# Tails of the second expert layer on the two partition halves of TensorE

## What is computed

```python
scores = jax.nn.softmax(xf @ gate_w.T, axis=-1)
_, idx = lax.top_k(scores + gate_b, 2)            # 2 of 8 experts for each of 4096 tokens
h = jax.nn.silu((einsum('td,edh->teh', xf, w1) + b1) * (einsum('td,edh->teh', xf, w3) + b3))   # h is 176 wide
oe = jnp.einsum('teh,ehd->ted', h, w2) + b2
y = jnp.einsum('te,ted->td', rw, oe)              # weighted by the two chosen scores
z = _expert(xf, sw1, sb1, sw3, sb3, sw2, sb2)     # one more expert of the same shape, for all tokens
x = x + y + z
```

## Time and profile before

| | |
|---|---|
| median of three runs | 703.93 us (702.35 to 705.06) |
| profiled execution, first to last instruction | 699.0 us |
| TensorE matmul busy | 653.6 us, 94% |
| TensorE weight load busy | 550.9 us, 79% |
| DVE / ACT / POOL busy | 527.0 / 421.3 / 507.5 us |
| mean granted TensorE clock | 0.978 |

### The profile page before, as it was taken

How to read it: one execution, slowest core, us unless ns; L and a number is a source line. 1 busy time by engine, 2 the same in 40 slices (tenths; PEclk the granted TensorE clock), 3 DMA queues, 4 the chain that set the end, 5 groups by cost and what they waited for, 6 DMA issues and landing times.

```text
span 699.0 us, 20550 instructions
## 1 busy us (share of the span) xinstructions
PE 653.6 (94%) x6836; PEld 550.9 (79%) x6836; DVE 527.0 (75%) x1507; ACT 421.3 (60%) x1166; POOL 507.5 (73%) x844
## 2 busy tenths in 40 slices
PE   8899999999988999999988999999899787999998
PEld 6577777777766999999985777777676676999997
DVE  4589999999853566665445789999999578778876
ACT  5567777776545333333444667677674675777773
POOL 5865588668765898887767776888787776777671
PEclk9999999999989999999997999999999999999999
DMA  5490001011423332334311101011121013333375
GB/s 178 112 352 6 10 26 33 26 33 35 159 68 93 116 119 62 95 97 126 88 41 35 32 17 32 29 59 46 35 71 49 32 48 98 103 100 101 94 251 195
DMA packets 45404, 57.69 MB, mean 83 GB/s; under 512 B 11379, under 2 KB 37142, under 8 KB 44630
## 3 DMA queue, kind: packets, MB, share of 16 engines
q1 hardware_dynamic: 36086, 38.12, 18.4%
q0 software_dynamic: 8640, 17.97, 7.6%
q10 hardware_dynamic: 576, 0.29, 0.2%
HBM read 33.77 MB, written 22.08 MB: 80 GB/s over the span
## 4 chain that ended last, share of the span: by engine, by line
PE 38%; DVE 23%; POOL 20%; issue 11%; DMA 2%; ACT 2%; SPq 2%; DVEq 0%; POOLq 0%; ACTq 0%
POOL results L1624 10%; PE S L2059 6%; PE ptp L2078 6%; DVE mx L1061 5%; DVE pr L1062 5%; PE M L1365 4%; PE S L1328 4%; POOL rows L620 3%; PE ptp L1348 3%; PE S L1330 3%; POOL xi L1617 3%; PE M L1416 2%; PE S L2065 2%; PE ptp L1351 2%; SPq L709 1%
## 5 line engine op out<-in xcount | busy, mean ns | idle before, releaser
L620 POOL DMA_INDIRECT rows<-out_rows,posi x128 | 126.9, 991 | 48.5 <-issue 28.5
L803 ACT ACTIVATE pT<-ptp 128x512 f32<-128x512 f32 (+1 forms) x192 | 94.1, 524 | 79.4 <-PE ptp L1348 72.3
L1061 DVE TENSOR_REDUCE mx<-S 128x16 f32<-128x1232 f32 x64 | 91.2, 1425 | 16.4 <-PE S L1330 15.8
L1624 POOL DMA_INDIRECT results<-early,xi x71 | 74.8, 1053 | 31.3 <-DVE early L1688 24.1
L1062 DVE TENSOR_TENSOR pr<-S,mx 128x1232 f32<-128x1232 f32 x64 | 92.2, 1441 | 2.2
L1929 POOL DMA_INDIRECT results<-early,xs x71 | 69.2, 975 | 27.4 <-issue 17.1
L1714 PE MATMUL S<-early,w1s 128*128 128x128 f32 x568 | 77.6, 280 | 5.0 <-DVE w1s L1681 3.3
L1724 PE MATMUL S<-first_w,early 128*128 x568 | 75.6, 276 | 0.7 <-DVE early L1688 0.7
L1714 PEld LDWEIGHTS S<-early,w1s 128*128 128x128 f32 x568 | 70.3, 195 | 7.6 <-issue 6.1
L1660 ACT ACTIVATE early<-S 128x128 f32<-128x128 f32 x71 | 19.6, 276 | 84.3 <-PE S L1707 84.3
L1688 DVE TENSOR_SCALAR early<-S,xs 128x128 f32<-128x128 f32 x71 | 24.9, 350 | 60.0 <-PE S L1724 33.2
(11 more groups left out here) (222 smaller groups left out, 1556.5 us busy)
## 6 DMA issues: line engine op xcount, KB each, us to landing
xs<-rows SPq DMA_DIRECT2D x142, 66.0 KB, 1.8
first_w<-in_e_W SPq DMA_DIRECT2D x2, 2048.0 KB, 8.5
swap<-results SPq DMA_DIRECT2D x32, 128.0 KB
first_w<-results SPq DMA_DIRECT2D x6, 512.0 KB, 7.9
rows<-out_rows,posi POOLq DMA_INDIRECT x128, 2.3
x_res<-in_x SPq DMA_DIRECT2D x1, 1536.0 KB, 8.6
W1r<-in_e_W SPq DMA_DIRECT2D x1, 1536.0 KB, 10.9
out_x<-x_res SPq DMA_DIRECT2D x3, 512.0 KB, 3.8
```

The source lines that it names most:

```text
L620: nc.gpsimd.indirect_dma_start(rows[:, :], bass.IndirectOffsetOnAxis(posi[:, k, n:n + 1], 0), out_rows[:, ring_slot(groups, n), k, :], Non ...
L803: nc.scalar.activation(pT[0:rows_of, G * r:G * r + count, :], ptp[q % 2][0:rows_of, 0:count, :], ACT.Exp, scale=SCALE)\
L1061: do(V.tensor_reduce(mx[:, :].rearrange("p (g j) -> p g j", g=G), sc, AX.X, ALU.max))
L1624: nc.gpsimd.indirect_dma_start(results[:, :], bass.IndirectOffsetOnAxis(xi[:, s:s + 1], 0), ys[:, s, :], None)\
```

## The change

- The tails of w1 and of w3 become products of their own, 64 output columns wide (L2098 of the new kernel). Tile 0's land on partitions 0 to 63, tile 1's on partitions 64 to 127 of the same 128 PSUM columns, so the w1 parts of a unit (2 x 128 of heads and 128 of tails) fill 384 columns of one bank, and the w3 parts 384 of another. TensorE runs them in tiles of 128 rows x 64 columns of its array.
- `c_copy`, `hidden` and `silu` of a routed unit become one instruction of 384 columns each. Shared units keep two in `c_copy` and `hidden` (the bias differs), of 256 and 128 columns.
- `narrow` makes the head products of both tiles (128 rows, L2112), then the two tail products of 64 rows each (L2117), tile 0 from partitions 0 to 63, tile 1 from 64 to 127 (tiles of 64 rows x 128 columns of the array). The outputs of tile 0 lie in one bank, those of tile 1 in the other, for every unit: `narrow(u)` now waits for DVE's reading of unit u - 1.
- w2's tail is laid out twice, on both halves. For tile 1 of a routed unit DVE copies it to a fixed place (`w2s`, L2002).
- `results_of` writes both tiles with one instruction (L2025).
- The bias row's factor of one now comes through the product: 1 x 1 through silu, so the rows of b2 are divided by silu(1) once, by three one-column instructions and one of 128 x 1152 on DVE in the first expert layer (`scale_bias_rows`, at its tile 12). POOL's memset goes.

The core of the diff:

```diff
         def widen(u):
-            wait(pe, hm_ready, 2 * u - 2)
-            bank, spare = S[:, 2 * (u % 2), :], S[:, 2 * (u % 2) + 1, :]
-            outs = (bank[:, 0:256], bank[:, 256:512], spare[:, 0:256])
...
-                for at, _ in enumerate(tiles_of(u)):
-                    for c, out in enumerate(outs):
-                        last = nc.tensor.matmul(out[:, at * 128:(at + 1) * 128], w1s[:, u % 2, at, c * 128:(c + 1) * 128],
-                                                xsT[:, r % 3, at, :], start=True, stop=True)
+                for at, own in enumerate(weights):
+                    for which in range(2):
+                        nc.tensor.matmul(inner(u, which)[:, at * 128:(at + 1) * 128], own[:, which * 128:(which + 1) * 128], moving[at],
+                                         start=True, stop=True)
...
+            for which in range(2):
+                for at, own in enumerate(weights):
+                    last = nc.tensor.matmul(inner(u, which)[TH * at:TH * (at + 1), 256:384], own[:, 256 + TH * which:256 + TH * (which + 1)],
+                                            moving[at], start=True, stop=True, skip_group_check=True)
             last.then_inc(up_ready, 1)
         def narrow(u, of):
             pe.wait_ge(hT_ready, u + 1)
-            if is_routed(u - 2):
-                pe.wait_ge(ys_ready, tiles_through(u - 2))
+            if is_routed(u - 1):
+                pe.wait_ge(ys_ready, units_through(u - 1))
...
+            for at in range(size):
+                nc.tensor.matmul(yp(u)[:, at, :], hT[:, u % 2, at * 128:(at + 1) * 128], w2[at][:, 0, :], start=True, stop=False,
+                                 skip_group_check=True)
+            for at in range(size):
+                rows_of = slice(TH * at, TH * (at + 1))
+                w2_tail = w2s[rows_of, routed_before(u) % 4, :] if of and at else w2[at][rows_of, 1, :]
+                last = nc.tensor.matmul(yp(u)[:, at, :], hT[rows_of, u % 2, 256:384], w2_tail, start=False,
+                                        stop=not with_planes(u), skip_group_check=True)
...
     def yp(u):
-        return ptp[u % 2][:, 0:2, :]
+        return both_ptp[:, 0:UNITS[u][2], 0, :]
...
         def c_copy(u):
-                nc.scalar.activation(head(cs, u), ac(u, 1), ACT.Copy).then_inc(cs_ready, 1)
-                nc.scalar.activation(tail(cs, u), tails(u, 64), ACT.Copy).then_inc(cs_ready, 1)
+                nc.scalar.activation(of_unit(cs, u), inner(u, 1)[:, 0:384], ACT.Copy).then_inc(cs_ready, 1)
...
         def silu(u):
-            nc.scalar.activation(head(hT, u), head(hm, u), ACT.Silu)
-            nc.scalar.activation(tail(hT, u), tail(hm, u), ACT.Silu).then_inc(hT_ready, 1)
+            nc.scalar.activation(of_unit(hT, u), of_unit(hm, u), ACT.Silu).then_inc(hT_ready, 1)
...
+        def scale_bias_rows():
+            one, bsh, tails = st["of_one"], st["bsh"], st["W2_1"][:, :, 1, :]
...
+            V.tensor_scalar(tails, tails, one[:, 2:3], None, ALU.mult).then_inc(w2_scaled, 1)
```

More of the change, by code:

```diff
@@ L41 @@
 X0, IDX, WGT = 1, D + 1, D + 2
-TAILF = F1 - 128
+TAILF, TH = F1 - 128, 64
 CW = 3 * 128
@@ L1828, in pairs_through, with inner, of_unit, parts_through @@
         return len([1 for what, _, _ in UNITS[:max(u, -1) + 1] if what == "shared"])
[L1830 to L1846, removed]
+    def inner(u, which):
+        return S[:, 2 * (u % 2) + which, :]
+    def of_unit(t, u):
+        return t[:, u % 2, 0:3 * 128]
+    def parts_through(u):
+        return sum(1 if what == "routed" else 2 for what, _, _ in UNITS[:max(u, -1) + 1])
+    def units_through(u):
+        return len([1 for what, _, _ in UNITS[:max(u, -1) + 1] if what == "routed"])
     def xTp(r):
@@ L1880, in load @@
             sp.wait_ge(xsT_ready, before // 2 + 1)
-            sp.wait_ge(ys_ready, before + 1)
+            sp.wait_ge(ys_ready, before // 2 + 1)
             sp.wait_ge(ys_out[before % U], 16 * (before // U) + 16)
@@ L1981, in w1_copies @@
                 e = expert(dve, i)
+                if at:
+                    r = routed_before(u)
+                    if r >= 4:
+                        dve.wait_ge(yp_ready, [v for v in range(NU) if is_routed(v)][r - 4] + 1)
+                    V.tensor_copy(w2s[:, r % 4, :], W2[:, bass.ds(e, 1), 1, :].rearrange("p a d -> p (a d)"))
                 V.tensor_copy(w1s[:, u % 2, at, :], W1r[:, bass.ds(e, 1), :].rearrange("p a f -> p (a f)")).then_inc(w1_copied, 1)
@@ L2015, in add_results @@
             xb = x[:, b0:b0 + HU, :]
-            steps.then(dve, V.tensor_tensor(xb, xb, yg[:, 0, b0:b0 + HU, :], ALU.add))
+            V.tensor_tensor(xb, xb, yg[:, 0, b0:b0 + HU, :], ALU.add).then_inc(x_done, 1)
+            dve.wait_ge(x_done, 2 * half + 1)
             V.tensor_tensor(xb, xb, yg[:, 1, b0:b0 + HU, :], ALU.add).then_inc(x_done, 1)
         dve.wait_ge(st["w1_less"], E)
+        st["keys_spread"](dve)
         halves = 0
@@ L2063, in widen @@
                 shared_turned(pe, b + 1)
-                for c, out in enumerate(outs):
-                    last = nc.tensor.matmul(out, W1s[:, c * 128:(c + 1) * 128], xall[:, b * T:(b + 2) * T], start=True, stop=True)
+                weights = [W1s[:, :]] * 2
+                moving = [xall[:, (b + at) * T:(b + at + 1) * T] for at in range(2)]
+                for which in range(2):
+                    nc.tensor.matmul(inner(u, which)[:, 0:256], W1s[:, which * 128:(which + 1) * 128], xall[:, b * T:(b + 2) * T],
+                                     start=True, stop=True)
+            for which in range(2):
+                for at, own in enumerate(weights):
+                    last = nc.tensor.matmul(inner(u, which)[TH * at:TH * (at + 1), 256:384], own[:, 256 + TH * which:256 + TH * (which + 1)],
+                                            moving[at], start=True, stop=True, skip_group_check=True)
             last.then_inc(up_ready, 1)
@@ L2175, in build @@
         sh["S"] = pb("S", [128, G, 512])
-        sh["ptp"] = [pb(f"ptp{i}", [128, J, T]) for i in range(2)]
+        sh["both_ptp"] = pb("ptp", [128, 2, J, T])
+        sh["ptp"] = [sh["both_ptp"][:, i, :, :] for i in range(2)]
         sh["M0"], sh["M1"] = pb("M0", [128, 512]), pb("M1", [128, 512])
```

110 lines of the change are left out of this document (65 added, 45 removed).

## The result

| | before | after |
|---|---|---|
| median of 4 runs, us | 704.49 (702.35 to 707.18) | 730.96 (729.69 to 731.32) |
| span of the profiled execution, us | 699.0 | 729.0 |

The ratio is 1.0366, with an interval of 1.0327 to 1.0404: 26.5 us slower by the medians, 30.0 by the spans. In the profiles of after (730.89) and of all experiments the execution's own time is 1.8 to 2.1 us above its span. By that measure the execution behind the profile of before took some 701, about 3.5 us less than its median. So of the 30.0, about 3.5 belong to the execution that was profiled and not to the change.

A forecast was written before the change was run, and what follows sets the result against it. The prediction took TensorE alone to bound the kernel from 589.5 us on. Its terms, 23.5 + 2.3 + 0.6 + 0.7 + 0.5 = +27.6 us, took the median from 703.93 to 731.5 us; own range 721 to 737.

The forecast's parts named there:

- Switches: TensorE after 589.5 us: four changes of tile size a unit, less `narrow`'s saved passes, cost +23.5 us (+17.8 to +25.2).
- back 0.22: Price in us of TensorE's return from 64-column or 64-row tiles to the full array, read in attention.
- The end: At the very end the last `narrow` waits for the addition of the one before: +0.6 us.
- The first routed unit: Single output buffer: `narrow(5)` waits for DVE's reading of unit 4, delaying the first routed `widen`: +2.3 us.
- The start: From 553 to 575 us, TensorE gets 3.3 us more work and ACT 2.3 less: +0.7 us (-2 to +3).
- First experts: Bias scaling in DVE's queue, three one-column instructions and one of 128 x 1152: +0.5 us (0 to 2).
- Rival 1: TensorE's switches are hidden and the kernel gets faster, POOL taking over: 699 us; chance 0.08.
- rival 2: TensorE's switches cost a quarter, about 0.2 us a unit: about 706 us; chance 0.04.
- Rival 3: The halves on TensorE's array don't go side by side: 760 us; chance 0.03.
- Rival 4: The single output buffer binds in every unit, DVE coming late: 13 us more, 745 us; chance 0.05.

The follow-up runs named there:

- e2: The changed kernel with `narrow`'s tail products over all 128 rows, so no 64-row tiles: 719.33 us, ratio 1.0261.
- e4: The changed kernel with each of `widen`'s four tail products writing all 128 output partitions, so no 64-column tiles: 736.32 us, ratio 1.0485.
- e1: The changed kernel with two buffers of outputs and tail products of 128 rows for units 0 to 5: 724.06 us, ratio 1.0334.
- e5: The changed kernel with eight unread products in each of the two places where TensorE idles around `narrow(5)`: 728.08 us, ratio 1.0367.
- e7: The changed kernel without the scaling of b2's rows in the first expert layer: 727.75 us, ratio 1.034.
- e8: The kernel before with one unread product of 64 rows and 128 moving columns ahead of each `narrow`: 732.9 us, ratio 1.0414.
- e10: The kernel before with the outputs of all units in one bank, so `narrow(u)` waits for unit u - 1; no switches: 708.22 us, ratio 1.0074.
- e3: The changed kernel with `widen(u)`'s tails between heads and tails of `narrow(u - 2)` from unit 11 on, three switches for four: 737.67 us, ratio 1.049.
- e9: The changed kernel with tail products of 128 rows and two buffers of outputs in all units: 715.92 us, ratio 1.0148.
- e6: The changed kernel with `widen`'s four tail products ordered tile by tile, both products of one tile together: 731.19 us, ratio 1.0391.
- e12: e11 with the second of TensorE's two register loads of a unit moved behind `narrow`'s heads: 725.63 us, ratio 1.03.
- e11: e3 with DVE doing `results_of(u - 2)` ahead of `hidden(u)` from unit 11 on: 731.78 us, ratio 1.0377.

## Why the prediction was right

The forecast was 731.5 us and the median 730.96; slower by over 0.5% had 0.88. The terms one by one:

**Switches, +23.5 predicted.** The rule held: each change of tile size costs about what attention's rows show. Routed unit 3.00 predicted, 2.92 measured, and e2 and e4 put the two parts at +0.30 and +0.17 where the sum had +0.36 and +0.19. Of the prices, into 64 columns (0.15) and into 64 rows (0.19 against 0.20) stand; back from 64 rows is 0.20, not 0.22. The weak step is "back 0.22" behind the 64-column tails: it was taken from a switch back to float32 weights in attention (those of the two passes of L1416, from 389.66, which the earlier trace rows leave out; the L1417 shown behind them has bf16), and costs 0.15 in front of `take` and 0.19 in front of `narrow`. From first send to end the prediction had 24.1 with the end's wait; the traces differ by 22.3. Units 0.47 to 0.51 longer, 42 to 44 of them, make about 21 of it, and the end 1.2 to 1.5.

**The end, +0.6 predicted, 1.2 measured as idle time, 1.5 from start to start.** The prediction saw one `narrow` that waits for the addition before it. There are two, 0.60 and 0.61 us idle, since only L2123 stands between the `narrow` of one of the last units and the next.

**The first routed unit, +2.3 predicted.** The wait is there, for the row that was named (1.90 us), and e1 shows that it and what comes with it are all of that stretch's growth. The wait itself is 2.35 (e5 less e1), of which up to 0.3 may be the switches that e1 leaves out. What the prediction left out is TensorE's clock at 1.2 GHz from 578.81 to 589.05 us, 1.8 more; it said that the clock "is no term", having read it in a stretch that lies behind this one.

**The start, +0.7 predicted:** 14.12 - 13.45 = 0.67 between the two table loads. The closeness is luck: the prediction picked 0.7 out of -2 to +3 without a sum for it. In this piece TensorE is busy for 12.80 us, 11.28 before, and ACT for 8.43, 10.78 before, so both moved the way that was said.

**First experts, +0.5 predicted (0 to 2), 0.9 measured** between POOL's first and last send (e7). DVE's work itself was 0.89 us for the 1152 columns, where the prediction had about 1 to 2.9. Of the 2.8 us by which the traces differ ahead of the second experts, this is one part. The larger one, 1.9, lies ahead of the first experts, in attention that the change leaves as it is: ACT's table load behind it stands at 216.34 before and at 218.20 after, and in the fourteen profiles anywhere from 214.5 to 218.2. That is a difference of executions.

The sum of what the traces show behind the second experts' start is 0.7 + 4.2 + 22.3 = 27.2, against 27.1 without the last term. That agreement is closer than it deserves: the switches were 1.8 too dear (with the end's second wait already in), and the clock, which wasn't in the sum, gave it back. The median has a second such pair. It was forecast as a span of 726.6 and 4.9 us from there to the median; measured are 729.0 and 2.0. The 4.9 was how far one execution of the kernel before lay below its median, and no part of the kernel's time; taken from median to median, +27.6 was forecast and +26.5 measured. *Rival 1* and *rival 2* fall by e2, e4 and e8: no switch was hidden, and a switch cost what attention's rows say. *Rival 3* falls by the pairs 0.01 us apart; for the columns also by e4 (0.89 one behind the other, 0.59 in pairs), for the rows by e8, where two passes behind a switch take 0.42 as the four of L2117 do. *Rival 4* falls by e10, and e3 shows the point from which it would have decided.

**Left open.** Why TensorE fell to 1.2 GHz. It had idled for 1.96 us just before in the changed kernel and 2.30 in e1, which kept 2.4 GHz; e9, which has no wait there, fell all the same from 578.17 to 581.58. What the fourteen profiles show is that the wait and a long fall of the clock go together: in all nine where `narrow(5)` waits and nothing fills the idle time, the clock is at half for 6.8 to 10.2 us around there, and in the other five for 3.4 (e8, e9) or not at all (before, e1, e5). The wait isn't shown to be the only cause, nor its absence a sure cure. The 64-row tails together with two buffers of outputs weren't tried: their outputs take both banks, and with two buffers in those DVE would read a bank that TensorE writes.

## What to carry to other kernels

Count changes of tile size in TensorE's queue before counting passes: here each cost 0.15 to 0.20 us with float32 weights of up to 128 columns, so that a pair of switches is worth three to four passes of 128 columns, and `narrow`'s pair saved two. Such a price can be read off a timeline of another part of the same kernel, but the way back depends on what follows, so read it before the weights that will follow. Where an extra buffer is given up, look at the two places where the pipeline fills and drains; the steady state may not show the wait at all.

## What was not expected of the hardware

- Products on the two halves run beside each other in both orders that were tried: L2098 stays at 0.59 us in e6, with both products of a tile together.
- Going from one split to the other, from 64 columns straight to 64 rows, costs 0.20 us, as much as coming from the full array: it is one switch and not two, but no cheaper one (e12).
- Loads of registers in TensorE's queue, 0.31 and 0.32 us each, cost nothing where they are behind 0.6 us of passes and 0.26 behind 0.22 us of them (e11: 0.71 for a piece of 0.45).
- One send of POOL beside DVE's 0.89 us on 1152 columns took 1.47 to 1.50 us in seven of ten profiles and 0.98 in three; it took 0.98 or 0.99 in all four without that work (e7).
- At 1.2 GHz the eight passes of L2086 take 1.92 us, at 2.4 GHz 1.06.
